# A gated delta-rule attention layer with a ternary feed-forward network on one core: the projection's softmax split over the steps, its products, copies and taps issued by half tiles, and two scale vectors loaded one stage earlier

## Chip, cores and metric

One core of a Trainium2 chip runs the whole kernel in one launch. The metric is the device time of that launch in microseconds; lower is better.

## What is computed

The input x is 4 sequences of 2048 tokens with 256 features. An attention layer with a residual and a layer norm is followed by a feed-forward network with a residual and a layer norm. Cut to what matters here:

```python
def _short_conv(x, w):                       # four taps over time, then silu
    xp = jnp.pad(x, ((0, 0), (K - 1, 0), (0, 0)))
    y = sum((xp[:, j:j + l, :] * w[:, j] for j in range(K)))
    return jax.nn.silu(y)

q = _short_conv(hidden_states @ Wq.T, conv_q)          # likewise k and v_direct
beta = jax.nn.sigmoid(hidden_states @ Wb.T)
delta_out = _delta_rule_chunkwise(q, k, v_direct, beta)       # chunks of 32 tokens, a triangular solve in each
local_s, local_m, local_l = (_fir(v_direct, f) for f in (fir_s, fir_m, fir_l))
logits = jnp.einsum('bld,hpd->blhp', hidden_states, gate_w) + gate_b
probs = jax.nn.softmax(logits / temp, -1)                     # five paths a head
probs = probs * (1.0 - 5.0 * eps) + eps
o = probs[..., 0:1] * local_s + probs[..., 1:2] * local_m + probs[..., 2:3] * local_l + probs[..., 3:4] * delta_out + probs[..., 4:5] * v_direct
attention = _rmsnorm(o, norm_w).reshape(b, l, H * DV) @ Wo.T

h = silu((x @ w1.T) * s1) * ((x @ w2.T) * s2)                 # 256 -> 1024
h = gelu((h @ h1.T) * hs1); h = gelu((h @ h2.T) * hs2)        # 1024 -> 1024, twice
out = (h @ w3.T) * w3_s                                       # 1024 -> 256
```

## The kernel before

Five engines run their own instruction lists and meet by semaphores only. Four stages follow each other, with all engines joined between them.

1. `project` (to about 367 us in the profiled execution): 16 steps of 128 tokens of all four sequences. Each step has six blocks `cb` of 128 features (two each of queries, keys, values). For a block TensorE multiplies (`products`, L295) into `proj[cb % 2]`, which takes two banks of the PSUM, two sequences in each; ScalarE writes the copy scaled with the fourth tap into `acc[cb % 3]` (L413); VectorE adds the three other taps in place, one after the other (`convolution`, L466); ScalarE applies silu (L382) into `yT`, which SP stores. `products` of a block waits until VectorE is done with the block two before.
2. `weights_fir` (to about 575 us): the FIR filters as matmuls, and the second half of the triangular solves.
3. `delta` (to about 910 us): the recurrence over the chunks. While it runs, the feed-forward weights are loaded and rounded; a flag says whether the rounding was exact.
4. `ffn`: each engine reads the flag (`either`, L1516) and branches; then three layers for each of 16 tiles.

Between the blocks of a projection step come pieces of the step before it. TensorE: after block 0 the keys are turned and multiplied (`keys`, L304, L321), after block 2 the gates and norms (`small`, L331, L338), after block 4 the values are turned (`values`, L304). VectorE: after block 2 it copies gates and norms out (`small_copies`, L473, L474), after block 4 the values (`values_out`, L481) and sums the key squares (L485). GpSimd squares queries and keys (L555, L561), and for half of the sequence solves the triangular systems in columns (`early_columns`, L155, L159), some in each step of a table (`EARLY_COLS`).

Three of the four quarters of the softmax over paths are done in this stage. After steps 4, 8 and 12 VectorE does the biased, scaled logits and subtracts their maxima (`first_logits`), and for two of the quarters the scales of the triangular systems (`first_scales`); ScalarE takes the exponentials at the end of the same step; one step later VectorE divides (`first_shares`). Each operation there waits for the one before it (`link`).

The scale vectors of the feed-forward network, `scol` and `srow`, are loaded by SP at the start of the last stage; ScalarE and VectorE wait for both before they do anything there.

## Time and profile before

| | |
|---|---|
| median of 3 runs | 2244.57 us (2244.39 to 2247.52) |
| profiled execution: time, span | 2240.09 us, 2238.3 us |
| TensorE busy | 2050.4 us, 92% of the span |
| VectorE busy | 1161.4 us, 52% |
| ScalarE busy | 875.1 us, 39% |
| GpSimd busy | 535.1 us, 24% |
| mean granted clock of TensorE | 0.963 |

Busy shares are means over stages with different limits. The profile's span is from the first to the last instruction; the time of the execution is 1.8 us longer. A duration of an instruction reaches to its last write, so that two neighbours can overlap a little.

### The profile page before, as it was taken

To read this page: it belongs to the slowest core of one execution; us is meant where nothing else is said; L and a number is where in the kernel's file an instruction comes from. 1 tells how busy PE (TensorE), PEld (TensorE's weight loads), DVE (VectorE), ACT (ScalarE), POOL (GpSimd) and SP (SyncE) were. 2 spreads that over 40 slices of the span, in tenths; PEclk is the share of its full clock that TensorE was granted. 3 is DMA by queue.
4 is the path that set the end of the run, shared out by engine and by line. 5 is a ranking of instruction groups with operands and counts; after the bars stand their busy time and mean duration, and the time that the engine had idled before them with its cause. 6 is when DMAs were issued, how large, how long until landed. Compare 5 with 4: busy or idle time off the path is not lost.

```text
span 2238.3 us, 42120 instructions
## 1 busy us (share of the span) xinstructions
PE 2050.4 (92%) x17462; PEld 1741.1 (78%) x17462; DVE 1161.4 (52%) x1836; ACT 875.1 (39%) x1418; POOL 535.1 (24%) x628
## 2 busy tenths in 40 slices
PE   6887876875899999799999999999999999999998
PEld 5766665775888887588888888888888888888886
DVE  5878786885467676424434434433443443443442
ACT  4444443102344444334434433443443443443442
POOL 1237872885455555000000000000000000000000
PEclk9989997987799999899999999999999999999999
DMA  6655555987999996100000000000000000000000
GB/s 180 192 155 167 175 159 164 299 260 227 199 220 242 228 229 171 37 1 29 1 29 29 6 23 29 29 1 29 29 1 29 29 1 29 29 1 29 29 1 19
DMA packets 250623, 208.81 MB, mean 93 GB/s; under 512 B 159634, under 2 KB 215378, under 8 KB 247890
## 3 DMA queue, kind: packets, MB, share of 16 engines
q1 hardware_dynamic: 238162, 175.84, 29.0%
q10 hardware_dynamic: 12288, 30.41, 4.8%
q8 instruction: 139, 2.28, 0.4%
q14 instruction: 34, 0.28, 0.0%
HBM read 126.32 MB, written 75.76 MB: 90 GB/s over the span
## 4 chain that ended last, share of the span: by engine, by line
PE 57%; issue 1%; DVE 1%; ACT 1%; DMA 0%; ACTq 0%; POOLq 0%; DVEq 0%; SPq 0%; POOL 0%
PE B L1622 50%; PE O L1649 5%; PE T L1580 1%; DVE yb L1755 0%; ACT gate L1694 0%; DMA srow<-in_srow 0%; DVE stats L1817 0%; ACT L1694 0%; DVE z L1808 0%; DVE z L1812 0%; DVE xl L1735 0%; DVE z L1831 0%; POOLq L1522 0%; ACT xh L1682 0%; ACTq L1516 0%
## 5 line engine op out<-in xcount | busy, mean ns | idle before, releaser
L1708 ACT ACTIVATE yb<-B,scol 128x512 f32<-128x512 f32 x256 | 176.6, 690 | 580.3 <-PE B L1622 580.3
L1622 PE MATMUL B<-act1l,wr 128*128 128x512 f32 x1024 | 398.4, 389 | 0.0
L1622 PE MATMUL B<-act0h,wr 128*128 128x512 f32 x1024 | 398.3, 389 | 0.0
L1622 PE MATMUL B<-act0l,wr 128*128 128x512 f32 x1024 | 398.3, 389 | 0.0
L1622 PE MATMUL B<-act1h,wr 128*128 128x512 f32 x1024 | 398.3, 389 | 0.0
L1743 DVE TENSOR_TENSOR act0l<-yb,act0h 128x512 fp32r<-128x512 f32 x256 | 176.1, 688 | 317.3 <-ACT act0h L1711 315.1
L295 PE MATMUL proj<-xt,w_qkv 128*128 128x262 f32 x768 | 203.4, 414 | 74.8 <-DVE acc L466 61.6
L466 DVE SCALAR_TENSOR_TENSOR acc<-proj,taps,acc 128x512 f32<-128x512 f32 x288 | 213.9, 749 | 82.6 <-ACT acc L413 74.4
L1743 DVE TENSOR_TENSOR act1l<-yb,act1h 128x512 fp32r<-128x512 f32 x128 | 88.6, 692 | 295.5 <-ACT act1h L1711 295.5
L295 PEld LDWEIGHTS proj<-xt,w_qkv 128*128 128x128 f32 x768 | 147.5, 201 | 116.8 <-DVE acc L466 69.8
L1622 PEld LDWEIGHTS B<-act1l,wr 128*128 128x128 f32 x1024 | 192.2, 188 | 39.9
L1622 PEld LDWEIGHTS B<-act0l,wr 128*128 128x128 f32 x1024 | 192.2, 188 | 39.9
L1622 PEld LDWEIGHTS B<-act0h,wr 128*128 128x128 f32 x1024 | 192.2, 188 | 39.9
L1622 PEld LDWEIGHTS B<-act1h,wr 128*128 128x128 f32 x1024 | 192.2, 188 | 39.9
L1622 PE MATMUL B<-xh,wr 128*128 128x512 f32 x512 | 202.6, 396 | 11.1 <-DVE xl L1735 6.9
L1864 POOL TENSOR_TENSOR rstd<-mv,ln_eps 128x4 f32<-128x4 f32 x16 | 3.2, 200 | 876.0 <-DVE mv L1825 876.0
L1622 PE MATMUL B<-xl,wr 128*128 128x512 f32 x512 | 200.9, 392 | 0.0
L1755 DVE SCALAR_TENSOR_TENSOR yb<-B,scol,gate 128x512 f32<-128x512 f32 x128 | 94.8, 749 | 177.3 <-ACT gate L1694 121.8
L781 PE MATMUL conv<-toe,win 128*128 128x192 f32 x512 | 131.0, 419 | 37.9 <-DMA toe<-in_toe_short 16.4
L781 PEld LDWEIGHTS conv<-toe,win 128*128 128x128 f32 x512 | 124.0, 315 | 44.7 <-DMA toe<-in_toe_short 18.8
L1622 PEld LDWEIGHTS B<-xh,wr 128*128 128x128 f32 x512 | 97.0, 189 | 37.0 <-DVE yb L1755 10.1
L1694 ACT ACTIVATE gate<-B,scol 128x512 f32<-128x512 f32 x128 | 86.7, 688 | 66.9 <-PE B L1622 66.8
(177 smaller groups left out, 3174.3 us busy)
## 6 DMA issues: line engine op xcount, KB each, us to landing
qk_s<-yT SPq DMA_DIRECT2D x16, 1024.0 KB, 5.1
qk<-qk_s SPq DMA_DIRECT2D x32, 512.0 KB, 4.7
wraw<-in_ffn_w ACTq DMA_DIRECT2D x32, 352.0 KB, 4.9
toe<-in_toe_short ACTq DMA_DIRECT2D x32, 320.0 KB, 7.4
xt<-in_xt SPq DMA_DIRECT2D x16, 524.0 KB, 4.2
toe<-in_toe_long ACTq DMA_DIRECT2D x32, 256.0 KB, 6.0
kk_s<-kfull SPq DMA_DIRECT2D x16, 512.0 KB, 5.1
k_s<-ktok SPq DMA_DIRECT2D x16, 512.0 KB, 6.0
```

Of the source, the lines that this page charges most:

```text
L295: last = nc.tensor.matmul(proj[cb % 2][:, 2 * half:2 * half + 2, 0:XW], w_qkv[:, k, cb * P:cb * P + P], xt[p][:, k, 2 * half:2 * half + 2, ...
L466: nc.vector.scalar_tensor_tensor(out=acc[cb % 3][:, :, :], in0=proj[cb % 2][:, :, j:j + P], scalar=taps[:, cb, j:j + 1], in1=acc[cb % 3][: ...
L781: last = nc.tensor.matmul(conv[n % 2][:, c // 2, c % 2 * NF * WIN:(c % 2 + 1) * NF * WIN], win[h % 2][:, :, g * FCH + c], toe[part % NTOE] ...
L1580: last = nc.tensor.transpose(T[:, k, b * P:b * P + P], x1[p][:, b, k * P:k * P + P], ident)
L1622: last = nc.tensor.matmul(B[slot % 4][:, :], w, part, start=(k == 0 and i == 0), stop=(k == kts - 1 and i == len(parts) - 1))
L1649: last = nc.tensor.matmul(O[:, b, :], sets[0][i][:, k, b * P:b * P + P], wr[:, W3 + k * D:W3 + k * D + D], start=(k == 0 and i == 0), stop ...
L1694: nc.scalar.activation(gate[m % 2][:, :], B[2 * m % 4][:, :], ACT.Silu, scale=scol[:, m:m + 1]).then_inc(gate_done, 1)
L1708: last = nc.scalar.activation(dst, B[slot % 4][:, :], ACT.Gelu, scale=scol[:, slot:slot + 1])
L1743: nc.vector.tensor_tensor(sets[s][1][:, m, :], yb[n % 3][:, :], sets[s][0][:, m, :].bitcast(f32), ALU.subtract).then_inc(lo_done, 1)
L1755: nc.vector.scalar_tensor_tensor(out=dst, in0=B[(2 * m + 1) % 4][:, :], scalar=scol[:, HT + m:HT + m + 1], in1=gate[m % 2][:, :], op0=ALU. ...
L1864: nc.gpsimd.tensor_tensor(rstd[:, :], mv[:, :, 1:2].rearrange("p b o -> p (b o)"), ln_eps[:, :], ALU.add).then_inc(rs_link, 1)
```

## The change

Three parts. (1) `products`, the scaled copy and each tap are done by halves, two of the four sequences (one bank of the PSUM) at a time, with a semaphore count for each half; the taps of the two halves alternate. Matmuls are the same and in the same order. (2) The softmax is cut into `first_logits`, `first_maxima`, `first_sums` and `first_shares`, which stand inside the steps t = 5, 9, 13 and two steps later, between blocks; `first_scales` stands at the end of steps 6 and 10, and the exponentials on ScalarE in steps 6, 10, 14 ahead of the copy of block 3. The turning of the scales on TensorE and its copies come two steps later than before, and GpSimd's columns one step later. (3) `scol` and `srow` are loaded by SP near the end of `delta`, into buffers that live through both stages.

```diff
-EARLY_COLS = {6: (0, 1, 8), 7: (0, 8, 14), 8: (0, 14, 20), 9: (0, 20, 31),
-              10: (1, 1, 8), 11: (1, 8, 14), 12: (1, 14, 20), 13: (1, 20, 27), 14: (1, 27, 31)}
+EARLY_COLS = {7: (0, 1, 8), 8: (0, 8, 14), 9: (0, 14, 20), 10: (0, 20, 31),
+              11: (1, 1, 8), 12: (1, 8, 14), 13: (1, 14, 20), 14: (1, 20, 26), 15: (1, 26, 31)}
...
                 def products(t, p, cb):
 
-                    pe.wait_ge(conv_done, t * CB + cb + 1)
+
                     for half in range(2):
+                        pe.wait_ge(conv_done, 2 * (t * CB + cb) + half + 1)
                         for k in range(KT):
                             last = nc.tensor.matmul(
                                 proj[cb % 2][:, 2 * half:2 * half + 2, 0:XW], w_qkv[:, k, cb * P:cb * P + P],
                                 xt[p][:, k, 2 * half:2 * half + 2, :], start=(k == 0), stop=(k == KT - 1))
-                    last.then_inc(proj_ready, 1)
+                        last.then_inc(proj_ready, 1)
...
+                def exponentials(t):
+
+                    c = t // PART_STEPS - 1
+                    if c in range(PARTS - 1) and t % PART_STEPS == 2:
+                        act.wait_ge(to_exp0, c + 1)
...
-                        nc.scalar.activation(acc[cb % 3][:, :, :], proj[cb % 2][:, :, HALO:XW], ACT.Copy,
-                                             scale=taps[:, cb, HALO:CONV]).then_inc(tap_done, 1)
+                        if cb == 3:
+                            exponentials(t)
+                        for half in range(2):
+                            act.wait_ge(proj_ready, 2 * (t * CB + cb) + half + 1)
+                            if cb >= 3 and half == 0:
+                                act.wait_ge(silu_done, t * CB + cb - 2)
+                            nc.scalar.activation(acc[cb % 3][:, 2 * half:2 * half + 2, :],
+                                                 proj[cb % 2][:, 2 * half:2 * half + 2, HALO:XW], ACT.Copy,
+                                                 scale=taps[:, cb, HALO:CONV]).then_inc(tap_done, 1)
...
                 def convolution(t, cb):
-                    dve.wait_ge(tap_done, t * CB + cb + 1)
+
                     for j in range(HALO):
...
+                        for half in range(2):
+                            if j:
+                                dve.wait_ge(conv_step, (t * CB + cb) * 2 * (HALO - 1) + 2 * (j - 1) + half + 1)
+                            else:
+                                dve.wait_ge(tap_done, 2 * (t * CB + cb) + half + 1)
+                            rows_of = slice(2 * half, 2 * half + 2)
+                            nc.vector.scalar_tensor_tensor(
+                                out=acc[cb % 3][:, rows_of, :], in0=proj[cb % 2][:, rows_of, j:j + P], scalar=taps[:, cb, j:j + 1],
+                                in1=acc[cb % 3][:, rows_of, :], op0=ALU.mult, op1=ALU.add,
+                            ).then_inc(conv_step if j < HALO - 1 else conv_done, 1)
...
                 def step(t, p, n, follow):
+
+                    c = (t - 1) // PART_STEPS - 1
+                    at = (t - 1) % PART_STEPS if c >= 0 else None
                     for cb in range(CB):
                         convolution(t, cb)
+                        if at == 0 and cb == 1:
+                            first_logits(c)
+                        if at == 0 and cb == 2:
+                            first_maxima(c)
+                        if at == 1 and cb == CB - 1 and c < EARLY:
+                            first_scales(c)
+                        if at == 2 and cb == 1:
+                            first_sums(c)
+                        if at == 2 and cb == 2:
+                            first_shares(c)
...
+                sp.dma_start(keep["scol"][:, :], io["scol"]).then_inc(keep["par_in"], 16)
+                src = io["srow"]
+                sp.dma_start(keep["srow"][:, :], bass.AP(tensor=src.tensor, offset=0, ap=[[0, P], [1, D]])).then_inc(keep["par_in"], 16)
```

VectorE around the first softmax quarter, before: the last block of step 4, then all of `first_logits` and `first_scales`, then block 0 of step 5.

```order
L466 SCALAR_TENSOR_TENSOR acc2<-proj1,taps,acc2 128x512 x3
L500 TENSOR_SCALAR eps<-prm 128x4
L501 TENSOR_SCALAR slope<-eps 128x4
L605 TENSOR_TENSOR lg0<-raw,prm 128x320
L607 TENSOR_TENSOR lg0<-lg0,itemp 128x320
L609 TENSOR_REDUCE mx0<-lg0 128x64
L610 TENSOR_TENSOR lg0<-lg0,mx0 128x320
L513 TENSOR_SCALAR ssk0<-kk 128x64
L516 TENSOR_SCALAR ebeta<-ebeta 128x64
L517 TENSOR_TENSOR half0<-ssk0,ebeta 128x64
L518 RECIPROCAL half0<-half0 128x64
L635 COPY gam0<-half0 128x8x4 x2
```

Now, at the same kind of place (the second quarter, step 9, whose rows are those of the first without `eps` and `slope`): block 1, the logits, block 2, the maxima, then the small copies and block 3.

```order
L476 SCALAR_TENSOR_TENSOR acc1<-proj1,taps,acc1 128x256 x6
L629 TENSOR_TENSOR lg0<-raw,prm 128x320
L631 TENSOR_TENSOR lg0<-lg0,itemp 128x320
L476 SCALAR_TENSOR_TENSOR acc2<-proj0,taps,acc2 128x256 x6
L636 TENSOR_REDUCE mx0<-lg0 128x64
L637 TENSOR_TENSOR lg0<-lg0,mx0 128x320
L520 TENSOR_SCALAR ssk0<-kk 128x64
L483 COPY raw<-side0 128x4x24
L484 COPY raw<-side1 128x4x4
L476 SCALAR_TENSOR_TENSOR acc0<-proj1,taps,acc0 128x256 x6
```

Three taps of 512 elements have become six of 256, and what stood in one run after block 5 stands after blocks 1 and 2 of the next step; the last four groups of it come a step later still, after block 5.

SP at the end of `delta`, before: the loads of the first feed-forward tile, three stores, the flag, the branches into the last stage, and there the two vectors.

```order
L1064 DMA x10<-y_s 128x1024
L1065 DMA xres5<-in_x 128x4x256
L1032 DMA y_s<-y1 128x512
L1032 DMA y_s<-y0 128x512
L1032 DMA y_s<-y1 128x512
L1069 DMA flag_s<-flag 1x1
L999 UNCONDITIONAL_BRANCH
L1523 UNCONDITIONAL_BRANCH
L1566 DMA scol<-in_scol 128x32
L1568 DMA srow<-in_srow 128x256
```

Now:

```order
L1098 DMA x10<-y_s 128x1024
L1099 DMA xres5<-in_x 128x4x256
L1100 DMA scol<-in_scol 128x32
L1102 DMA srow<-in_srow 128x256
L1066 DMA y_s<-y1 128x512
L1066 DMA y_s<-y0 128x512
L1066 DMA y_s<-y1 128x512
L1106 DMA flag_s<-flag 1x1
L1033 UNCONDITIONAL_BRANCH
```

The two loads stand ahead of the last three stores and of the flag.

## Rows read from the trace of the kernel before

**Rows 1.** Stretches: us busy of PE, PEld, DVE, ACT, POOL; granted clock, DMA share, GB/s.
```profile
14.00:110.00 96.00, 82.79 (x894) 66.40 (x894) 75.87 (x106) 45.86 (x72) 16.88 (x9) 1.00 0.56 173
110.00:130.00 20.00, 15.65 (x116) 12.36 (x109) 12.07 (x26) 10.23 (x17) 3.75 (x2) 0.66 0.47 153
```

**Rows 2.** Timeline of VectorE: start, us, instruction, idle before it and releaser.
```profile
60.75 0.25 DVE L473 COPY raw<-side 128x96 f32<-128x96 f32 x1
...
62.44 4.55 DVE L466 SCALAR_TENSOR_TENSOR acc<-proj,taps,acc 128x512 f32<-128x512 f32 x6 [1.36 <-ACT acc L413]
...
69.17 2.32 DVE L466 SCALAR_TENSOR_TENSOR acc<-proj,taps,acc 128x512 f32<-128x512 f32 x3
72.90 4.79 DVE L466 SCALAR_TENSOR_TENSOR acc<-proj,taps,acc 128x512 f32<-128x512 f32 x6 [1.42 <-ACT acc L413]
78.07 2.32 DVE L466 SCALAR_TENSOR_TENSOR acc<-proj,taps,acc 128x512 f32<-128x512 f32 x3 [0.38 <-ACT acc L413]
80.31 0.25 DVE L473 COPY raw<-side 128x96 f32<-128x96 f32 x1
...
345.63 0.25 DVE L473 COPY raw<-side 128x96 f32<-128x96 f32 x1
...
904.16 1.41 DVE L1404 BATCH_NORM_STATS2 stats<-x 128x6 f32<-128x256 f32 x4
```

**Rows 3.** Timeline of ScalarE in the same step.
```profile
61.72 0.69 ACT L413 ACTIVATE acc<-proj,taps 128x512 f32<-128x512 f32 x1 [2.72 <-PE proj L295]
...
71.52 0.63 ACT L382 ACTIVATE yT<-acc 128x512 f32<-128x512 f32 x1 [3.42 <-DVE acc L466]
72.18 0.69 ACT L413 ACTIVATE acc<-proj,taps 128x512 f32<-128x512 f32 x1
```

**Rows 4.** Timeline of TensorE in that step, in a disturbed one, and at 910 us.
```profile
59.65 3.80 PE L295 MATMUL proj<-xt,w_qkv 128*128 128x262 f32 x16
...
75.28 2.03 PE L295 MATMUL proj<-xt,w_qkv 128*128 128x262 f32 x8 [1.71 <-DVE acc L466]
...
142.90 3.55 PE L295 MATMUL proj<-xt,w_qkv 128*128 128x262 f32 x8 [2.83 <-DVE acc L466]
...
910.78 1.94 PE L1580 MATMUL T<-const,x 128*128 128x128 f32 x8 [3.10 <-PEq L999]
```

**Rows 5.** The line of the small copies, over the whole execution.
```profile
L473 DVE COPY raw<-side x16: 247/247/258, 41.4 to 362.7; 128x96 f32<-128x96 f32 x16
```

**Rows 6.** VectorE's groups in 100 to 366 us: busy us, mean ns | idle.
```profile
L607 DVE TENSOR_TENSOR lg<-lg,itemp 128x320 f32<-128x320 f32 x3 | 3.1, 1021 | 0.1
...
L500 DVE TENSOR_SCALAR eps<-prm 128x4 f32<-128x4 f32 x1 | 0.2, 159 | 0.0
```

**Rows 7.** Groups of one shape each, whole execution: busy us, mean ns | idle.
```profile
L466 DVE SCALAR_TENSOR_TENSOR acc<-proj,taps,acc 128x512 f32<-128x512 f32 x288 | 213.9, 749 | 82.6 <-ACT acc L413 74.4
...
L146 DVE TENSOR_TENSOR tri<-tri,neg_gamT 128x512 f32<-128x512 f32 x1 | 0.7, 683 | 0.0
...
L146 DVE TENSOR_TENSOR tri<-tri,neg_gamT 128x256 f32<-128x256 f32 x1 | 0.4, 417 | 0.0
...
L1230 ACT ACTIVATE us<-XY 128x512 f32<-128x512 f32 x31 | 18.5, 598 | 10.9 <-PE XY L1130 10.9
...
L1235 ACT ACTIVATE oT<-TW 128x256 f32<-128x256 f32 x32 | 12.3, 384 | 34.6 <-PE TW L1170 34.6
```

**Rows 8.** Timeline of GpSimd around its longest bundle of columns.
```profile
217.13 0.97 POOL L155 TENSOR_TENSOR outer<-tri 128x440 f32<-128x440 f32 x1
...
238.46 1.90 POOL L555 TENSOR_TENSOR sq<-yT 128x1024 f32<-128x1024 f32 x1
```

**Rows 9.** The chain that ended last, in order of time: start, us, what.
```profile
911.16 4.69 DMA srow<-in_srow
...
917.30 1.03 ACT xh L1682
...
919.64 74.99 PE B L1622 x320
```

More of the change, by code:

```diff
@@ L341, in small @@
                     c = t // PART_STEPS - 1
-                    if c in range(EARLY) and t % PART_STEPS == 0:
+                    if c in range(EARLY) and t % PART_STEPS == 2:
                         pe.wait_ge(ktok_out, t + 1)
@@ L352, in values @@
                     c = t // PART_STEPS - 1
-                    if c in range(EARLY) and t % PART_STEPS == 0:
+                    if c in range(EARLY) and t % PART_STEPS == 2:
                         pe.wait_ge(gam0_out, 2 * c + 2)
@@ L380, in silu @@
                 def silu(t, p, cb):
-                    act.wait_ge(conv_done, t * CB + cb + 3)
+                    act.wait_ge(conv_done, 2 * (t * CB + cb) + 6)
                     nc.scalar.activation(yT[p][:, cb, :].rearrange("p (b n) -> p b n", b=BATCH),
                                          acc[cb % 3][:, :, :], ACT.Silu).then_inc(silu_done, 1)
+                def exponentials(t):
+                    c = t // PART_STEPS - 1
+                    if c in range(PARTS - 1) and t % PART_STEPS == 2:
+                        act.wait_ge(to_exp0, c + 1)
+                        if c < EARLY:
+                            act.wait_ge(small_out, (c + 1) * PART_STEPS + 1)
+                            if c:
+                                act.wait_ge(gam0_done, c)
+                            nc.scalar.activation(ebeta[:, :, :], raw[:, c * NE:c * NE + NE, NGATE:NGATE + HEADS], ACT.Exp,
+                                                 scale=-1.0).then_inc(exp0_done, 1)
+                        nc.scalar.activation(lg0[:, :, :, :], lg0[:, :, :, :], ACT.Exp).then_inc(exp0_done, 1)
                 def scales_out(t):
                     c = t // PART_STEPS - 1
-                    if c in range(EARLY) and t % PART_STEPS == 0:
+                    if c in range(EARLY) and t % PART_STEPS == 2:
                         act.wait_ge(gam0_turned, c + 1)
@@ L452, in _ @@
                 dve.wait_ge(prm_in, 16)
-                dve.sem_inc(conv_done, 2)
+                dve.sem_inc(conv_done, 4)
                 dve.sem_inc(small_out, 1)
@@ L460, in convolution @@
                 def convolution(t, cb):
-                    dve.wait_ge(tap_done, t * CB + cb + 1)
                     for j in range(HALO):
-                        if j:
-                            dve.wait_ge(conv_step, (t * CB + cb) * (HALO - 1) + j)
-                        nc.vector.scalar_tensor_tensor(
-                            out=acc[cb % 3][:, :, :], in0=proj[cb % 2][:, :, j:j + P], scalar=taps[:, cb, j:j + 1],
-                            in1=acc[cb % 3][:, :, :], op0=ALU.mult, op1=ALU.add,
-                        ).then_inc(conv_step if j < HALO - 1 else conv_done, 1)
+                        for half in range(2):
[8 more added lines that the diff above has]
+                            ).then_inc(conv_step if j < HALO - 1 else conv_done, 1)
                 def small_copies(t):
@@ L503, in first_logits, with first_maxima @@
                     dve.wait_ge(small_out, (c + 1) * PART_STEPS + 1)
[L504 to L508 removed]
+                    gate_logits(nc, link, keep, lg0, rows(c))
+                def first_maxima(c):
+                    gate_maxima(nc, link, lg0, mx0).then_inc(to_exp0, 1)
+                    if c < EARLY:
+                        dve.wait_ge(kk_summed, (c + 1) * PART_STEPS + 2)
+                        nc.vector.tensor_scalar(ssk0[:, :, :].rearrange("p (t b) h -> p t (b h)", b=BATCH),
+                                                kk[:, c * PART_STEPS:(c + 1) * PART_STEPS, :], L2_EPS, None, ALU.add)
                 def first_scales(c):
[L512 to L514 removed]
                     dve.wait_ge(exp0_done, 2 * c + 1)
@@ L599, in early_rows, with gate_logits @@
     sub.scaled_rows().then_inc(keep["inv_done"][0], 1)
-def gate_logits(nc, link, keep, lg, mx, rows):
+def gate_logits(nc, link, keep, lg, rows):
     temp = bcast(bcast_mid(keep["itemp"][:, :], rows.stop - rows.start), 5)
@@ L610, in gate_logits, with gate_sums @@
     return nc.vector.tensor_tensor(lgf, lgf, bcast(mx[:, :], 5), ALU.subtract)
-def gate_shares(nc, link, keep, lg, mx, rows):
+def gate_sums(nc, link, keep, lg, mx, rows):
     n = rows.stop - rows.start
@@ L620, in gate_shares @@
     link(nc.vector.tensor_tensor(by_head, by_head, bcast_mid(keep["slope"][:, :], n), ALU.mult))
+def gate_shares(nc, link, keep, lg, mx, rows):
+    n = rows.stop - rows.start
+    lgf = lg[:, :, :, :].rearrange("p t h f -> p (t h) f")
     link(nc.vector.tensor_tensor(lgf, lgf, bcast(mx[:, :], 5), ALU.mult))
@@ L1469, in ffn @@
     with outer.ctx:
-        scol = outer.sb("scol", [P, 4 * HT])
-        srow = outer.sb("srow", [P, D])
+        scol, srow = keep["scol"], keep["srow"]
         power = outer.sb("power5", [P, BATCH])
@@ L1926, in build @@
                     ("stats1", 6), ("mv1", 2), ("rstd1", 1)))
-                keep["x1_in"] = late.pair("p5_x_in")
+                keep["scol"], keep["srow"] = late.sb("scol", [P, 4 * HT]), late.sb("srow", [P, D])
+                keep["x1_in"], keep["par_in"] = late.pair("p5_x_in"), late.sem("p5_par_in")
                 for n in ("xres_in", "x1_sum", "st1_done", "var1_done", "rs1_link", "rstd1_done", "x1_ready"):
```

41 lines of the change are left out of this document (10 added, 31 removed).

## The prediction

> **What bounds the kernel now.** I read the stages first, then one undisturbed step of the projection stage, then its disturbed steps, then the chain that ended last. From 919.64 us on that chain is TensorE, nearly back to back; the change touches nothing there but its start. Ahead of it lies the wait for the small vector `srow`, 4.69 us [rows 9]. The rest of the change is in the projection stage, whose first and last `small_copies` start at 41.4 and 362.7 us [rows 5]. No engine is full there: in 14 to 110 us TensorE is busy 82.79 of 96 and VectorE 75.87 [rows 1]. They work in a ring: product, scaled copy on ScalarE, three taps on VectorE, and the product two blocks later waits for the last tap. One step shows where the waits are: small copies to copies is 80.31 - 60.75 = 19.56 us, with idle stretches of 1.36 ahead of block 3, 1.42 ahead of block 0, and 0.38 ahead of block 2; a fourth of 0.15 sits inside the run of 4.79 that holds blocks 0 and 1 [rows 2]. Together 3.3 us a step.
>
> **Disturbed steps.** 41.4 to 362.7 is 321.3 us. Fourteen periods of 19.56 and the last one of 17.1 (345.63 to 362.7) make 290.9 [rows 2, 5]; so 30.4 us are extra in the six steps with softmax work. The work itself is sixteen groups, the costliest with 3.1 us, the least with 0.2, 23.2 us in all [rows 6]. It stands after block 5 each time, where it covers the 1.42 us that VectorE would wait anyway: six times, 8.5 us. That leaves 14.7 us of work and 15.7 us of something else. The granted clock tells what: TensorE waits long behind these pieces, and then the share is 0.66 in 110 to 130 us, against 1.00 in 14 to 110 [rows 1]; at a share of 0.5 the clock is 1.2 GHz, the lower of its two levels. After an idle of 2.83 us the eight matmuls at 142.90 took 3.55 us, where those at 75.28 took 2.03; the idle of 1.71 ahead of these, the longest in an ordinary step, lowered nothing [rows 4].
>
> **Term 1: halves, undisturbed step.** Cost first. A block of three dependent taps runs 2.32 us; starts lie (2.32 - 0.75) / 2 = 0.785 apart, and the last is followed by independent work 80.31 - 78.07 - 2 x 0.785 = 0.67 after its start [rows 2, 7]. So a tap of 512 elements holds the engine 0.67 when nothing depends on it, 0.12 more when the next one does. With two halves in turn the neighbour is always independent. What a half holds is not in the trace. Going from 512 to 256 elements takes 683 - 417 = 266 ns off an operation [rows 7]; so 0.67 - 0.27 = 0.40. It lasts 0.75 - 0.27 = 0.48 and the tap that needs it starts 0.80 later, so its wait is over by then. A block is 6 x 0.40 = 2.41 in place of 2.24: plus 0.17, 1.0 us a step. The bounds: below, four independent operations of 256 elements start (1.41 - 0.42) / 3 = 0.33 apart [rows 2, 7], 2.0 a block; above, each half exposes its whole length and the 0.035 that a waiting tap shows, 0.52, 3.1 a block. I take 0.40, since the row of the same instruction gives all but the 256 elements. The Trainium skill ("Perfetto Trace Analysis", Optimizing Scalar/DVE Operations) gives about 125 ns of overhead for a VectorE operation on PSUM; that would be 0.39, and the row's 0.67 agrees. Its page "VectorE: DVE Perf Modes" (the TRN2 errata) speaks against the change: pieces of 512 elements or more spread the fixed cost. By rows that is the 1.0 us just counted.
>
> What it buys: (a) Ahead of block 3: product 3 starts at 59.65, its copy at 61.72, the tap at 62.44 [rows 2 to 4]. With halves the copy of half 0 starts after about 1.2 (the second four of eight matmul records, 0.88 by 3.80 / 2 less the ends, fall away) and lasts about 0.47: a 128x256 copy is 598 - 384 = 214 ns shorter than 128x512 [rows 7], from 0.69 [rows 3]. The tap can start at 1.7, the second half's at 2.6. VectorE comes free at about 1.6. Wait 1.36 becomes about 0.5. (b) Ahead of block 0: the last tap ends at 71.49, the silu starts 71.52, the copy 72.18, the tap 72.90 [rows 2, 3]; only the copy gets shorter: 1.42 becomes 1.2. (c) The 0.38 and the 0.15: from the last tap of a half of block 0 to the first tap of block 2 is 0.06 + 1.2 + 0.47 + 0.03 = 1.8 us, under the 2.41 of block 1: gone, but for about 0.05. Sum 3.3 to 1.75, a gain of 1.55 against 1.0: **0.5 us a step, 8 us in sixteen**. TensorE is not in the way: 82.79 of 96 is 16.9 a step of 19.56, under 19.0. GpSimd's substitution columns move one step later. Their longest bundle runs from 217.13 to 238.46, 21.3 us, and two squarings of 1.9 follow [rows 8]: 25.1, against 19 a step. I price it at nothing, since what VectorE takes from GpSimd it takes late (the key sums after block 4, two thirds of a step behind the squarings' start); if that cover is gone, once in the stage, it is 25.1 - 19 = 6 us at most.
>
> **Term 2: softmax in pieces.** After: two operations after block 1, two or three after block 2, the scales after block 5 of the next step, the shares again after blocks 1 and 2. The work stays 23.2 us. What hides it: the 0.5 us ahead of block 3, in seven or eight pieces that stand just before it or one block earlier, about 2; the 1.2 ahead of block 0 for the two scales, 2.4. Left: 18.8 us. No piece is longer than about 3 us; laid into the step, TensorE's longest wait ahead of block 2 grows from 1.7 to some 2.2. I take it that the clock stays up, since 1.71 did nothing, and the 15.7 us go. The two exponentials on ScalarE, with a table load each way, now stand before the copy of block 3, where ScalarE waits 2.72 us for TensorE [rows 3]; with halves that wait shrinks to about 1.6, so they cost a few tenths, three times. The scales for the substitution come two steps later, and GpSimd's columns one step later with them. **30.4 to 18.8: 11.6 us.**
>
> **Term 3: vectors early.** Two issues of 0.4 us go ahead of the last three stores of `y`, which wait for results anyway; SP hides them. The landing at 911.16 + 4.69 = 915.85 falls away. ScalarE then reads the flag (from the landing to its copy at 917.30, 1.45 us) from 910.78 on, done at 912.2, and waits for the transposes, which end at 910.78 + 1.94 = 912.72 [rows 4, 9]. The copy starts at 912.75 in place of 917.30: **4.5 us**. TensorE's first matmul follows that copy by 919.64 - 917.30 = 2.34 us, so at 915.1; its own flag read, as long as ScalarE's, fits before it. The next thing late is the transposes.
>
> **Sum.** 8 + 11.6 + 4.5 = 24. The profiled run took 2240.1 (span 2238.3); the median is 2244.6, 4.5 higher, and I take the difference from it: 2220.5.
>
> **The rivals.**
> *Cheap halves.* A half holds VectorE 0.33, the lower bound: 2.0 a block, 2.4 us a step less than in term 1; then TensorE (16.9) and the waits around block 0 bound the step at about 17.6: 31 us in term 1, so 2244.6 - 31 - 16.1 = 2197. For it: the 0.33 row. Against it: those read no PSUM and no scalar vector, and the tap's own 0.67 is 0.06 above 512 elements plus their fixed part. The skill's "Vector Engine (DVE) Microarchitecture Reference" (5.2) has about 75 ns fixed for every built-in operation, which would be 0.34 here; the tap row shows 0.135. 0.12.
> *The clock still falls.* Pieces of 2 to 3 us in nine steps in place of 4 us in six; TensorE waits ahead of block 2 while they run, and the clock had fallen after an idle of 2.83 us [rows 4]. If half or more of the 15.7 stays, or a piece holds up the ring more than counted: 2228 to 2238. 0.20.
> *Dear halves (the other side).* The wait of each half on a result two taps back stops the overlap, or the engine needs more than 0.40. VectorE is now what bounds the step (14.5 + 2.5 of other work + waits of 1.75), so every 0.01 us a half is 0.36 us a step, 5.8 in sixteen. All 24 us are gone at 0.44; at 0.52 it is 2244.6 + 45 = 2290, less what waits give back. For it: VectorE has the least slack of all; against it: satisfied waits show no gap in the 0.67. 0.11.
> *It does nothing.* Extra of halves at 0.43 to 0.45 eats the other two terms: within 0.2% of 2244.6. 0.07.
>
> **How the numbers follow.** The forecast has 0.50, and its own range is 2210 to 2230 (a half at 0.39 to 0.41, term 2 by 3 either way, the early part of the filter stage by 2). A measurement of this kernel tells 0.2%, 4.5 us. Faster: 0.50 + 0.12 + 0.20 = 0.82; same 0.07; slower 0.11. The range 2199 to 2244 leaves out nearly half of the cheap case below (0.05) and, above, dear halves and half of nothing (0.145).
>
> **What would show it.** Taps of 128x256 starting 0.40 apart and lasting 0.48, six in 2.4 us. Copies to copies 19.0 in undisturbed steps. Idle ahead of block 0 1.2, ahead of block 3 at most 0.5. Granted clock at 1.00 from 14 to 350 us. Nine disturbed steps that hold 19 us more. First matmul of the last stage 4.5 us after ScalarE's copy would have waited, that is 2.4 us behind the transposes. Wrong it would be by taps over 0.44 apart, by a clock below 0.9 in the stage, or by GpSimd late with the key squares around the tenth step.

## The result, and the profile after

| | before | changed |
|---|---|---|
| median of the runs beside each other | 2246.05 us (2244.39 to 2252.86) | 2215.74 us (2214.83 to 2219.19) |
| profiled execution: span | 2238.3 us | 2213.0 us |
| mean granted clock of TensorE | 0.963 | 0.971 |

The ratio is 0.9862, with a 95% interval of 0.9838 to 0.9886: 30.3 us less, where 24 were forecast. On another chip the changed kernel came out at 0.9860 (0.9834 to 0.9887; e10_after below).

First the stretches that [rows 1] show of before, from the changed kernel's trace (columns: busy us of TensorE's matmuls, of its weight loads, of VectorE, ScalarE and GpSimd, then the granted clock, the share of the DMA engines and GB/s):

```profile
14.00:110.00 96.00, 85.29 (x904) 68.97 (x904) 83.46 (x200) 54.54 (x107) 16.87 (x9) 1.00 0.60 180
110.00:130.00 20.00, 16.50 (x191) 13.46 (x192) 18.45 (x45) 9.60 (x20) 3.80 (x2) 1.00 0.56 182
130.00:345.00 215.00, 171.43 (x1986) 139.44 (x1984) 193.02 (x437) 116.79 (x227) 156.61 (x215) 0.97 0.58 181
```

VectorE is busy 83.5 of 96 us where it was 75.9, TensorE 85.3 where it was 82.8, and the clock of 110 to 130 us is 1.00 where it was 0.66. One undisturbed step on VectorE, the answer to [rows 2]:

```profile
59.56 0.24 DVE L483 COPY raw<-side 128x96 f32<-128x96 f32 x1
59.72 0.16 DVE L484 COPY raw<-side 128x16 f32<-128x16 f32 x1
59.96 0.48 DVE L476 SCALAR_TENSOR_TENSOR acc<-proj,taps,acc 128x256 f32<-128x256 f32 x1
60.84 4.40 DVE L476 SCALAR_TENSOR_TENSOR acc<-proj,taps,acc 128x256 f32<-128x256 f32 x11 [0.40 <-ACT acc L429]
65.16 1.22 DVE L491 COPY vtok<-tok 128x1024 f32<-128x1024 f32 x1
66.29 1.21 DVE L495 TENSOR_REDUCE kk<-sqk 128x16 f32<-128x1024 f32 x1
67.42 2.44 DVE L476 SCALAR_TENSOR_TENSOR acc<-proj,taps,acc 128x256 f32<-128x256 f32 x6
71.06 2.44 DVE L476 SCALAR_TENSOR_TENSOR acc<-proj,taps,acc 128x256 f32<-128x256 f32 x6 [1.20 <-ACT acc L429]
73.67 4.79 DVE L476 SCALAR_TENSOR_TENSOR acc<-proj,taps,acc 128x256 f32<-128x256 f32 x12 [0.17 <-ACT acc L429]
78.38 0.25 DVE L483 COPY raw<-side 128x96 f32<-128x96 f32 x1
```

Small copies to small copies is 78.38 - 59.56 = 18.82 us, against 19.56. Of block 3 one half tap starts at once, and VectorE waits 0.40 us before the next; 1.20 us stay ahead of block 0. Twelve half taps run in 4.79 us, so they start (4.79 - 0.48) / 11 = 0.392 us apart. TensorE's longest wait in this step is 1.61 us, where it was 1.71 [rows 4]. The stage, as the line of the small copies shows it (duration shortest/median/longest, first and last start), and the group of the taps:

```profile
L483 DVE COPY raw<-side x16: 243/248/258, 40.7 to 342.8; 128x96 f32<-128x96 f32 x16
L476 DVE SCALAR_TENSOR_TENSOR acc<-proj,taps,acc 128x256 f32<-128x256 f32 x576 | 232.7, 476 | 41.2 <-ACT acc L429 40.4
```

302.1 us from first to last against 321.3 [rows 5]. The taps' busy time grew from 213.9 [rows 7] to 232.7 us, and the idle time ahead of them fell from 82.6 to 41.2.

One step of the stage went badly. VectorE there (and, for comparison, the same two operations at 358 us), then GpSimd, then TensorE:

```profile
237.94 2.44 DVE L476 SCALAR_TENSOR_TENSOR acc<-proj,taps,acc 128x256 f32<-128x256 f32 x6
240.29 2.83 DVE L653 TENSOR_TENSOR lg<-lg,mx 128x320 f32<-128x320 f32 x1
243.15 2.27 DVE L654 TENSOR_TENSOR pw<-lg,eps 128x320 f32<-128x320 f32 x1
245.46 0.26 DVE L483 COPY raw<-side 128x96 f32<-128x96 f32 x1
...
358.13 0.49 DVE L653 TENSOR_TENSOR lg<-lg,mx 128x320 f32<-128x320 f32 x1
358.66 0.70 DVE L654 TENSOR_TENSOR pw<-lg,eps 128x320 f32<-128x320 f32 x1
```

```profile
239.13 3.64 POOL L162 TENSOR_TENSOR tri<-tri,gamT 128x2048 f32<-128x2048 f32 x1
242.74 2.13 POOL L579 TENSOR_TENSOR sq<-yT 128x1024 f32<-128x1024 f32 x1
244.84 2.23 POOL L585 TENSOR_TENSOR sqk<-ktok 128x1024 f32<-128x1024 f32 x1
```

```profile
238.05 4.02 PE L296 MATMUL proj<-xt,w_qkv 128*128 128x262 f32 x16
241.91 1.04 PE L305 MATMUL tok<-const,yT 128*128 128x128 f32 x8
247.81 6.61 PE L296 MATMUL proj<-xt,w_qkv 128*128 128x262 f32 x16 [4.86 <-DVE acc L476]
```

The two shares operations, 0.49 and 0.70 us at 358 us, lasted 2.83 and 2.27. The first began while GpSimd scaled rows, and it ended 0.35 us behind the end of that (243.12 against 242.77); the second ended 0.55 us behind the end of the first squaring (245.42 against 244.87). TensorE waited 4.86 us, and then its 16 matmuls took 6.61 us where they had taken 4.02. This step's period was 26.29 us (219.17 to 245.46).

The same happens in milder form in the other steps with softmax work. The subtraction of the maxima, 0.49 us at 354 us, took 1.04 us once and 1.40 twice, and the first shares operation 1.60 twice. Each of these five began while GpSimd squared and ended 0.34 or 0.35 us behind the end of that squaring; one of them:

```profile
198.73 1.40 DVE L637 TENSOR_TENSOR lg<-lg,mx 128x320 f32<-128x320 f32 x1
```

Six of the periods from small copies to small copies are long, 21.7 to 26.3 us, 25.7 us above six undisturbed ones in all. The period behind each of the first five is 18.17 us in place of 18.83, so 3.3 us come back and 22.4 us are left.

And the start of the last stage, the answer to [rows 4, 9]:

```profile
887.22 1.94 PE L1613 MATMUL T<-const,x 128*128 128x128 f32 x8 [3.10 <-PEq L1033]
894.59 0.77 PE L1655 MATMUL B<-xh,wr 128*128 128x512 f32 x1 [5.43 <-issue]
```

```profile
889.19 1.02 ACT L1715 ACTIVATE xh<-T 128x1024 fp32r<-128x1024 f32 x1 [4.52 <-PE T L1613]
```

```profile
890.43 1.23 DVE L1768 TENSOR_TENSOR xl<-T,xh 128x1024 fp32r<-128x1024 f32 x1 [5.90 <-ACT xh L1715]
```

ScalarE's copy comes right behind the transposes, as forecast. But `xl` is ready at 891.66, and the first matmul of `B` comes at 894.59. From the first transposes to it there were 919.64 - 910.78 = 8.86 us, and now 7.37.

**Where the 25.3 us between the two profiled spans came from.** The last reduction of `kk` marks the end of VectorE's work in the projection stage, before and now:

```profile
365.77 1.21 DVE L485 TENSOR_REDUCE kk<-sqk 128x16 f32<-128x1024 f32 x1
```

```profile
345.80 1.21 DVE L495 TENSOR_REDUCE kk<-sqk 128x16 f32<-128x1024 f32 x1
```

It ends 20.0 us earlier (347.01 against 366.98); from there to the first `Q` matmul of the delta stage (561.14 before, 539.46 now) 1.7 us less; from that to the end of the last stage's transposes 1.9 less (349.7 against 351.6); the start of the last stage 1.5 less, and 0.2 behind it. The medians differ by 30.3. The 5 us between are taken up under e3 to e13.

### The profile page after: what moved, and what is told of

The parts are those of the page before. It is cut to its first block, busy times and chain, and to the rows that moved or that the text cites. A ratio compares the mean times of both kernels' runs of the same rounds, so it can differ in the third digit from the quotient of the medians.

```text
span 2213.0 us, 42512 instructions
## 1 busy us (share of the span) xinstructions
PE 2037.1 (92%) x17462; PEld 1731.9 (78%) x17462; DVE 1184.3 (54%) x2124; ACT 894.1 (40%) x1514; POOL 535.0 (24%) x628
## 4 chain that ended last, share of the span: by engine, by line
PE 57%; issue 1%; DVE 1%; ACT 1%; POOLq 0%; DVEq 0%; ACTq 0%; POOL 0%
PE B L1655 51%; PE O L1682 6%; PE T L1613 1%; DVE yb L1788 0%; ACT gate L1727 0%; DVE stats L1850 0%; ACT L1727 0%; DVE xl L1768 0%; DVE z L1845 0%; DVE z L1841 0%; DVE z L1864 0%; POOLq L1558 0%; ACT xh L1715 0%; DVEq L1783 0%; ACTq L1726 0%
## 5 line engine op out<-in xcount | busy, mean ns | idle before, releaser
L296 PE MATMUL proj<-xt,w_qkv 128*128 128x262 f32 x768 | 195.7, 401 | 65.5 <-DVE acc L476 51.2
L476 DVE SCALAR_TENSOR_TENSOR acc<-proj,taps,acc 128x256 f32<-128x256 f32 x576 | 232.7, 476 | 41.2 <-ACT acc L429 40.4
L296 PEld LDWEIGHTS proj<-xt,w_qkv 128*128 128x128 f32 x768 | 142.2, 194 | 104.8 <-DVE acc L476 59.2
L1655 PEld LDWEIGHTS B<-xh,wr 128*128 128x128 f32 x512 | 96.9, 189 | 35.5 <-DVE yb L1788 10.2
```

The lines of the kernel that those rows point to most:

```text
L296: last = nc.tensor.matmul(proj[cb % 2][:, 2 * half:2 * half + 2, 0:XW], w_qkv[:, k, cb * P:cb * P + P], xt[p][:, k, 2 * half:2 * half + 2, ...
L476: nc.vector.scalar_tensor_tensor(out=acc[cb % 3][:, rows_of, :], in0=proj[cb % 2][:, rows_of, j:j + P], scalar=taps[:, cb, j:j + 1], in1=a ...
L1655: last = nc.tensor.matmul(B[slot % 4][:, :], w, part, start=(k == 0 and i == 0), stop=(k == kts - 1 and i == len(parts) - 1))
```

## The experiments

All ratios are to the kernel before on the same chip, with 95% intervals. Single runs scatter: the kernel before took 2228.9 to 2259.7 us in the 76 runs beside the experiments, the changed one 2204.8 to 2219.2 in ten. So stages are read from the profiled executions and the totals from the ratios.

**e1_halves**: the kernel before, with these edits of the change alone:

```diff
                     for half in range(2):
+                        pe.wait_ge(conv_done, 2 * (t * CB + cb) + half + 1)
...
+                        last.then_inc(proj_ready, 1)
...
+                            rows_of = slice(2 * half, 2 * half + 2)
```

> The kernel before with the half tiles alone: products, scaled copies and taps by halves, the softmax and the scale vectors where they were. Theory (the terms add): a step free of the softmax falls from 19.56 us to the 18.83 us of the changed kernel, so 16 steps give some 11.7 us, and the softmax keeps its long pauses and clock drops; 2246.1 - 11.7 = 2234, the last kk reduction near 355. Rival (the halves also take up the pauses, because TensorE runs half a tile less behind): about 2226, and then the pieces of the softmax are worth little. Second rival (the softmax in one piece costs more once a step is tighter, since it delays more steps): above 2238.

Measured: 0.9957 (0.9934 to 0.998), 9.6 us less. Small copies and clock:

```profile
L478 DVE COPY raw<-side x16: 243/247/258, 39.7 to 355.7; 128x96 f32<-128x96 f32 x16
```

```profile
110.00:345.00 235.00, 192.02 (x2032) 156.79 (x2032) 202.19 (x464) 122.63 (x241) 158.39 (x216) 0.90 0.54 167
195.96 3.86 PE L296 MATMUL proj<-xt,w_qkv 128*128 128x262 f32 x8 [6.88 <-DVE acc L471]
```

The undisturbed period is 18.82 us, as in the changed kernel. But from first to last it is 316.0 us: 14 x 18.82 and a last 16.7 leave 35.9 us extra, where before had 30.4. TensorE waited 6.88 us behind the softmax in one piece, and eight matmuls took 3.86 us afterwards. So the second rival holds in part: tight steps pay more for an undivided piece. The last `kk` reduction ended at 359.96, 7.0 us before that of the kernel before, where the theory had 355.

**e2_softmax**: the softmax in pieces and GpSimd's column table, with whole tiles and late vectors.

```diff
+                        if at == 0 and cb == 1:
+                            first_logits(c)
...
+                        if at == 2 and cb == 2:
+                            first_shares(c)
...
-                    if t % PART_STEPS == 0:
-                        first_logits(t // PART_STEPS - 1)
```

> The kernel before with the softmax in pieces alone (and the early columns of GpSimd moved with it), whole tiles. Theory (the terms add): the undisturbed step stays 19.56 us, the extra of the disturbed steps falls from 30.4 us towards the 22.4 us of the changed kernel, so 8 us less: 2238. By the prediction's own term, 11.6 us less: 2234.5. Rival (the pieces pay only with half tiles, since a piece between two whole blocks holds TensorE as long as before): 2244 to 2247.

Measured: 0.9956 (0.9935 to 0.9976), 9.9 us less.

The clock of 110 to 345 us before, and in this run:

```profile
110.00:345.00 235.00, 187.08 (x2026) 150.54 (x2019) 186.65 (x271) 108.89 (x174) 155.03 (x215) 0.92 0.54 167
```

```profile
110.00:345.00 235.00, 186.49 (x2136) 150.89 (x2125) 202.94 (x284) 114.98 (x184) 159.89 (x217) 0.98 0.56 173
L478 DVE COPY raw<-side x16: 243/247/258, 41.5 to 348.8; 128x96 f32<-128x96 f32 x16
```

307.2 us, less 14 x 19.55 and a last 15.7: 17.8 us extra against 30.4, so 12.6 less where the term said 11.6, and the clock is 0.98 where before has 0.92 and e1 0.90. The last `kk` reduction ended at 353.00, 14.0 us earlier than before. 7.0 + 14.0 = 21.0, and both together gave 20.0: in the stage the two parts add up. They meet in the disturbed steps, though: with halves the pieces leave 22.4 us extra (302.0 - 14 x 18.83 - 16.0), and without the pieces 35.9. The six long periods hold nearly the same extra in both, 25.3 us here and 25.7 in the changed kernel; what differs is the next period, which gives back 1.45 us here (18.10 in place of 19.55) and 0.66 there. That fits a VectorE with less slack. The two shares operations took 3.30 and 2.27 us in the worst step here too.

**e4_whole_taps**: the changed kernel, taps whole, products and scaled copies by halves. TensorE waits once for a block, since a whole tap frees both halves together. (A block has three taps and holds VectorE 2.24 us; "five" and "3.4 us" in the expectation are slips.)

```diff
-                        for half in range(2):
+                    dve.wait_ge(tap_done, 2 * (t * CB + cb) + 2)
...
-                                in1=acc[cb % 3][:, rows_of, :], op0=ALU.mult, op1=ALU.add,
+                            in1=acc[cb % 3][:, :, :], op0=ALU.mult, op1=ALU.add,
```

> The changed kernel with whole taps (128x512, five to a block), its products and scaled copies still by halves. Theory (what shortens the step is that a tap of the other half hides the 0.12 us that a dependent half tap would wait, and that block 0 and block 3 start on half a product): whole taps give a block of some 3.4 us less the time that they lose at its start, where VectorE waits for both copies; TensorE gets the bank back only when all four rows are done, so the period is between 18.8 and 19.6 us, near 19.3: 16 x 0.5 = 8 us above the changed kernel, 2223.7. Rival A (only the products and copies by halves count, the taps' form is the same): 2216. Rival B (VectorE alone bounds the step and whole taps are the cheaper form, 2.24 us against 2.35 a block, six blocks): 6 x 0.11 = 0.7 us a step less, 2205.

Measured: 0.9981 (0.9952 to 1.001), some 27 us above the changed kernel by the ratios, and none of the three numbers. The undisturbed step is 19.5 us, as with whole tiles throughout. The rest is the clock. TensorE in two steps that have no softmax in them:

```profile
74.87 2.03 PE L297 MATMUL proj<-xt,w_qkv 128*128 128x262 f32 x8 [1.86 <-DVE acc L474]
...
94.37 3.37 PE L297 MATMUL proj<-xt,w_qkv 128*128 128x262 f32 x8 [1.86 <-DVE acc L474]
```

```profile
14.00:110.00 96.00, 83.73 (x832) 66.70 (x830) 74.99 (x104) 52.09 (x102) 16.87 (x9) 0.98 0.56 171
110.00:345.00 235.00, 199.89 (x2007) 160.89 (x2007) 186.19 (x263) 120.13 (x235) 145.01 (x203) 0.87 0.54 163
```

After the second wait of 1.86 us the same eight matmuls took 3.37 us. Before has 1.71 us in this place and keeps 1.00 [rows 1, 4]; the changed kernel has 1.61. From 110 to 345 us the clock is 0.87, where e2 has 0.98. Half products and copies under whole taps go with a wait of TensorE that is 0.15 us longer, since the first tap starts only when both halves are copied; half taps take 0.25 off it again. This suggests that the ordinary step of before stood close to losing the clock. It is a reading of two kernels that differ in more than this wait, not a test of it.

**e8_halves_in_row**: the changed kernel, with the three taps of half 0 ahead of the three of half 1.

```diff
-                    for j in range(HALO):
-                        for half in range(2):
+                    for half in range(2):
+                        for j in range(HALO):
```

> The changed kernel with the three taps of half 0 first and then the three of half 1. Theory (a half tap holds VectorE 0.39 us, lasts 0.48, and one that depends on the tap just ahead waits for its end: starts 0.51 apart): a block takes 4 x 0.51 + 2 x 0.39 = 2.8 us in place of 2.35, six blocks 2.7 us a step; half of block 3's and block 0's waits are taken up by it, so the undisturbed step is 20.5 to 21.3 us against 18.83. Rival (a wait on the tap just ahead costs a half tap nothing, since the engine works in order anyway): 18.8, with a block of 2.35.

One run, 2253.3 us:

```profile
65.78 5.80 DVE L476 SCALAR_TENSOR_TENSOR acc<-proj,taps,acc 128x256 f32<-128x256 f32 x12
71.50 1.21 DVE L491 COPY vtok<-tok 128x1024 f32<-128x1024 f32 x1
72.63 1.21 DVE L495 TENSOR_REDUCE kk<-sqk 128x16 f32<-128x1024 f32 x1
73.76 2.94 DVE L476 SCALAR_TENSOR_TENSOR acc<-proj,taps,acc 128x256 f32<-128x256 f32 x6
```

```profile
14.00:110.00 96.00, 84.15 (x785) 63.53 (x785) 81.73 (x174) 47.47 (x93) 13.34 (x8) 0.92 0.50 152
```

Six taps run in 2.94 us in place of 2.44 and the undisturbed step takes 20.96 us: the theory's range. Four of the five starts in such a row depend on the tap just ahead: (2.94 - 0.48 - 0.39) / 4 = 0.517 us, 0.125 above the 0.392 of alternating halves. So the 0.12 us that a dependent tap waits is there for halves too; the alternation is what removes it. The clock is 0.92 in a stretch without softmax, though TensorE's longest single wait is 1.57 us: the longest wait alone doesn't tell when the clock falls. The many short waits between half products may count as well; no run separates them.

**e11_shares_next_step**: the changed kernel, with the shares of the first two quarters one step later. (e7_shares_later moved them for all three quarters and gave no time: the third quarter's would fall into a seventeenth step, and there are sixteen.)

```diff
-                        if at == 2 and cb == 2:
+                        if (at == 3 and cb == 1) if c < 2 else (at == 2 and cb == 2):
                             first_shares(c)
```

> The changed kernel with the shares of the first two quarters one step later, behind block 1 of the step after, away from the time in which GpSimd scales the rows of the early solve (the third quarter's stay). Theory (the period of 26.29 us is contention of VectorE and GpSimd for the same memory): that period falls to about 21, the two shares operations take 1.0 to 1.2 us in place of 2.83 and 2.27, the clock stays 1.00 until 340 us; 5 us less than e10_after. Rival (they are slow wherever they stand beside GpSimd's many small columns): the long period moves one step on and nothing is gained. Rival on the other side: a step that was free of softmax now has a piece, so 1 to 3 us more.

Measured: 0.9835 (0.9808 to 0.9862), beside e10_after at 0.9860 (0.9834 to 0.9887) on the same chip: 0.25% less, though the intervals overlap. The trace tells it more sharply:

```profile
254.58 0.48 DVE L653 TENSOR_TENSOR lg<-lg,mx 128x320 f32<-128x320 f32 x1
255.10 1.10 DVE L654 TENSOR_TENSOR pw<-lg,eps 128x320 f32<-128x320 f32 x1
```

```profile
237.45 3.65 POOL L162 TENSOR_TENSOR tri<-tri,gamT 128x2048 f32<-128x2048 f32 x1
241.06 1.89 POOL L579 TENSOR_TENSOR sq<-yT 128x1024 f32<-128x1024 f32 x1
242.91 1.89 POOL L585 TENSOR_TENSOR sqk<-ktok 128x1024 f32<-128x1024 f32 x1
```

The shares take 0.48 and 1.10 us, the squarings 1.89 each, the long period is 21.1 us where e10_after has 26.4 once more, and the last `kk` reduction ends at 341.75 against 347.27 in e10_after: 5.5 us, the theory's size. The expected clock did not come: 0.96 from 130 to 345 us in both. The second operation still takes 1.10 us where 0.70 is its time at 358 us in the changed kernel. So the long step was in the main two engines in each other's way. The Trainium skill ("SBUF — State Buffer", SBUF: two separate sides) has it that VectorE and GpSimd share one pair of ports as an exclusive lock: between a VectorE operation with two SBUF inputs and a GpSimd instruction that reads SBUF, the one that starts first keeps it for its whole length, and the other blocks. The rows agree: the stretched operations ended 0.35 and 0.55 us behind the GpSimd instruction that was running when they started.

**e3_vectors and e6_vectors_again**: the kernel before with the early scale vectors alone, twice.

```diff
+                sp.dma_start(keep["scol"][:, :], io["scol"]).then_inc(keep["par_in"], 16)
...
+                keep["scol"], keep["srow"] = late.sb("scol", [P, 4 * HT]), late.sb("srow", [P, D])
```

> The kernel before with the two scale vectors loaded early alone. Theory (TensorE needs some 5.4 us from the end of its transposes to its first matmul behind the flag, whatever the vectors do): the stretch from the first transposes of the feed-forward stage to its first matmul of B falls from 8.89 us to about 7.4, so 1.5 us less: 2244.5. The prediction's term: 4.5 us less, 2241.5. Rival (the two earlier loads get in the way of the loads that the end of the delta stage waits for): 2246 or more.

> The kernel of e3_vectors once more, on another set of runs. Theory (its gain is the 1.5 us of the trace): ratio 0.999, 1.5 us less than before, and the interval of e3 (0.9924 to 0.9975) was scatter. Rival (loading or placing the vectors early gives some 8 us more, in the delta stage): ratio 0.995 again.

Measured: 0.995 (0.9924 to 0.9975) and 0.9976 (0.9949 to 1.0004), so 11 and 5 us less. In both traces the first `B` matmul comes 5.4 us behind the end of the transposes, where it was 6.9: 1.5 us, by the theory. e3's ratio is more than that; e6's interval takes the theory's 0.999 in.

**e5_place_only**: the tiles of the two vectors and their semaphore where the change has them, the loads where before has them (the second line of the diff above without the first). **e9_no_vectors**: the changed kernel without that part. **e10_after**: the changed kernel again. **e13_loads_late**: the changed kernel with e5's form of the part.

> The kernel before with the two scale vectors' tiles and their semaphore placed where the changed kernel has them (ahead of the delta stage, which moves that stage's tiles in SBUF), but their loads issued where the kernel before issues them. It stands beside e3_vectors, whose runs came out some 11 us faster (0.5%) where its trace shows 1.5 us less at the start of the last stage. Theory (the place of tiles is nothing, and e3's further gain is the scatter of the delta stage, whose length differs by 15 us between profiled executions): 2246, ratio 1.000, and 6.9 us from the end of the last transposes to the first matmul of B. Rival (the other place of the delta stage's tiles makes that stage shorter): ratio near 0.996, with some 349 us from the first Q matmul to the last transposes where kernels with the old place have 352 to 364.

> The changed kernel without its early scale vectors: their tiles, semaphore and loads back where the kernel before has them; halves and pieces stay. Theory (the vectors' part is the 1.5 us of the start of the last stage): 1.5 us above the changed kernel, which runs beside it as e10_after. Rival (the place of the delta stage's tiles is worth some 5 us, as e5_place_only came out at 0.9974, and of the 30 us measured this part holds 6 to 7): 6 to 7 us above e10_after, and from the first Q matmul to the last transposes over 351 us in its profiled execution.

> The changed kernel as it is, to compare others with on the same chip and to see how its profiled execution scatters. Every theory: ratio 0.986 to the kernel before, 31 us less, within what repeats scatter (some 3 us). If its steps come again with a period near 26.3 us at the tenth step, with a TensorE idle of 4.9 us, the contention seen there is the kernel's and not chance.

> The changed kernel with the scale vectors' tiles where it has them, but their loads issued where the kernel before issues them. Theory (the place of the delta stage's tiles is worth some 6 us, the early loads only the 1.5 us between 6.92 and 5.43 us ahead of the first matmul of B): ratio 0.9867, 1.5 us above e10_after. Rival (the early loads are worth the whole 8 us by which e9_no_vectors came out above e10_after): ratio 0.9895, as e9. In the profiled execution the stretch from the last transposes to B is 6.9 us by both; from the first Q matmul to the last transposes it is near 349 us by the theory, as the mean of the kernels with the new place, and near 358 by the rival that the place is nothing, as the mean of the four with the old.

| | ratio | interval | first `Q` matmul to the end of the last transposes, us |
|---|---|---|---|
| before, e1, e2 (old place) | | | 351.6, 364.1, 356.5 |
| e9_no_vectors (old place) | 0.9895 | 0.9864 to 0.9925 | 359.1 |
| e10_after (new place) | 0.9860 | 0.9834 to 0.9887 | 339.9 |
| e13_loads_late (new place) | 0.9873 | 0.9843 to 0.9903 | 352.8 |
| e5_place_only (new place) | 0.9974 | 0.9953 to 0.9994 | 350.3 |
| after, e3, e4, e6, e8, e11, e12 (new place) | | | 349.7, 349.3, 351.9, 348.2, 342.5, 356.9, 352.8 |

The part of the vectors is worth 8 us by e9 against e10, whose intervals overlap, and e5 comes out faster than before although it loads nothing earlier. The delta stage takes 357.8 us in the mean of the four traces with the old place and 348.7 in that of the ten with the new one, with a spread of some 5 us in either group. (In e12 the transposes themselves come 7.2 us late, for the reason given there; without these its 352.8 is 345.5, and the mean takes this.) Two traces of the same changed kernel, after and e10_after, lie 9.8 us apart, though, as much as the groups do. The summed time of no group of VectorE, ScalarE or GpSimd operations differs between the two by over 0.4 us, so it is mostly waits that differ. So the place of the delta stage's tiles, which two more tiles ahead of them shift, is likely worth 5 to 8 us. Neither how it acts nor that it isn't chance in ten against four traces is shown. e13's 0.9873 lies between its two expectations, nearer to the theory's 0.9867, but its interval holds the rival's 0.9895 too, and so does its trace lie between 349 and 358.

**e12_flag_first**: the changed kernel with the flag read ahead of the transposes.

```diff
                 def emit(general):
+                    turn(0, 0)
                     if general:
...
-                turn(0, 0)
                 either(pe, emit)
```

> The changed kernel with TensorE's read of the flag, and the branch on it, ahead of the first transposes of the last stage, which stand in both branches then. In the changed kernel 5.43 us pass from the end of the transposes to the first matmul of B, though ScalarE and VectorE have its operand ready 2.5 us after that end. Theory A (what those 5.43 us hold is the flag read, some 3 us, and a start of the branch's code that must come after it): the transposes start 3 us later than before, end 2 us later still, and B follows the operand at once, 2.5 us on: 7.4 us in all from the start of the stage, the same as now: ratio to e10_after 1.000. Theory B (the read takes as long as ScalarE's, under 2 us, and the rest is code that is fetched only when the branch is taken, in either order): the sum grows to 2 + 1.9 + 2.5 and the fetch in between, up to 9.5 us, 2 us more than e10_after. Theory C (the matmuls issued ahead of the read hold it up until they are done): read and branch take 1.5 us from the stage's start, B follows 5.9 us after that start: 1.5 us less.

Measured: 0.9876 (0.985 to 0.9901), some 3.6 us above e10_after, with overlapping intervals. SyncE's first load of the last stage, which marks its start, in the changed kernel and in this one, and TensorE in this one:

```profile
887.18 0.36 SPq L1562 DMA_DIRECT2D x<-y_s  x1
```

```profile
882.56 0.36 SPq L1562 DMA_DIRECT2D x<-y_s  x1
```

```profile
889.81 1.97 PE L1613 MATMUL T<-const,x 128*128 128x128 f32 x8 [10.30 <-issue]
894.15 0.79 PE L1655 MATMUL B<-xh,wr 128*128 128x512 f32 x1 [2.37 <-DVE xl L1768]
```

The transposes start 7.25 us behind the stage's start, and `B` comes 11.59 behind it, where it came 7.41 in the changed kernel (887.18 to 894.59). So TensorE's read of the flag with its branch takes some 7.3 us from the stage's start, wherever it stands. Ahead of the transposes it is paid in full; behind them, its first 2 us lie under them. What the 7.3 us consist of is not shown. Of the three theories none had so long a read; B's direction, a loss, is the one that came.

## Why the prediction was right, and where it was off

**Term 1, 8 us forecast.** Half taps 0.39 us apart and 0.476 long, six in 2.44: the forecast was 0.40, 0.48, and 2.4. The waits ahead of block 0 (1.20) and block 3 (0.40, one tap in front of it) are as said. The step fell 0.73 us and not 0.5, to 18.83 where 19.0 was forecast: a block holds VectorE 6 x 0.392 = 2.35 us and not 2.41, 0.36 less in six, and the waits are 0.1 longer than said. Undisturbed steps alone make that 10.2 us in fourteen, but e1 gave 7.0 in the stage, since the undivided softmax cost more. The step "a half holds the engine 0.40, the independent neighbour hides the dependence" is shown from both sides by e4 and e8. The rivals of cheap and dear halves fell by the one number 0.392.

**Term 2, 11.6 us forecast.** The mechanism is shown by e2: pieces in place of one block, 12.6 us of the extra gone, and a clock of 0.98 from 110 to 345 us, where e1 has 0.90. In the changed kernel the extra is 22.4 where 18.8 was forecast, in six long periods and not in nine. The step that was mis-sized is "no piece is longer than about 3 us": the piece of the shares reached 245.42 from 240.29, 5.1 us, because it met GpSimd. The working had looked at GpSimd for columns that come late and not for what its long operations do to VectorE's. The sign was in [rows 6]: `L607` has a mean of 1021 ns, and the same operation takes 0.49 us where it is undisturbed (at 111.43 us in that trace). e11 takes 5.5 us back out of the stage.

**Term 3, 4.5 us forecast, 1.5 at the place it named.** ScalarE's copy moved just as forecast (1.97 us behind the start of the transposes, where it was 6.52). The step that failed is "its own flag read, as long as ScalarE's, fits before it": e12 puts TensorE's read and branch at 7.3 us. In the kernel before that had been hidden behind `srow` and what follows its landing, the copy and `xl`, which put the first `B` matmul 8.9 us behind the stage's start; with `srow` gone the read is what is late next.

**The sum.** 24 against 30.3. By the traces: 20.0 for terms 1 and 2 (19.6 forecast), 1.5 for term 3, and 3.6 between the projection stage and the last one that no term had. The rest, 5 us, is the difference between one pair of executions and the medians, and the place of the delta stage's tiles is the likely owner of it, not the shown one. So terms 1 and 2 came out near by their mechanism, while the total is near by luck in part: a gain that was not foreseen outweighed the 3 us that term 3 fell short.

**The rival "the clock still falls"** stood at 0.20. It came in small: 0.97 from 130 to 345 us. It lay near: in e4, where TensorE waits 1.86 us in each step in place of 1.61, the clock from 110 to 345 us is 0.87, and with the longer step nearly the whole gain is gone.

## What to carry to other kernels

Cutting a chain of dependent VectorE operations in two halves in turn held VectorE a little longer here, 2.35 us a block in place of 2.24; it paid because the next engine could begin on half a tile, and the waits of a step fell from 3.3 to 1.8 us. The same halves one after the other lost, at 2.94. Where TensorE waits in every step, a small change of its waits can go with a loss of clock in the whole stage (e4, e8), so an edit is to be judged with the granted clock of each stretch beside it. Before vector work is laid into a gap, look at what GpSimd runs at that time; and before a load is moved off the path, price what each engine still has to do there, its own reads and branches too.

The best version measured is e11_shares_next_step: 2209.1 us in the median, 0.9835 of before, against 2213.6 and 0.9860 of the changed kernel on the same chip; the two intervals overlap.

## What of the hardware was not expected

- A VectorE operation of 0.49 us lasted 2.83 (3.29 in e10_after's trace) beside a GpSimd tensor operation of 3.64 us, and the GpSimd squaring behind it 2.23 in place of 1.89.
- TensorE's read of a flag and the branch on it: 7.3 us from the stage's start to its next matmul. ScalarE's copy, behind its own read of the same flag, started 2.0 us after the stage's start.
- The same eight matmuls took 2.03 or 3.37 us after waits of the same length, 1.86 us, in two steps next to each other.
